# Attention scores in opposite 64-row halves, stacks filled head by head by transfers within SBUF, the maximum's row sent by ACT

## The reference

```
x = x + attention(layernorm(x))          # 16 heads of 16 channels, 512 tokens a sequence
q = xn @ Wq.T + bq + ocr_bias ; k = xn @ Wk.T + bk ; v = xn @ Wv.T + bv
scores = q @ k.T / 4 + band              # band: 0.1 where |i - j| <= 2
out = softmax(scores) @ v
return out @ Wo.T + bo
```

## Time and profile before

| | |
|---|---|
| Median of 3 runs | 4211.57 us (4206.95 to 4215.46) |
| The profiled execution | 4213.35 us, its span 4211.6 us |
| Attention stage, first to last score matmul | 2152.8 to 3442.4 us of the span |
| Busy: PE, PEld, DVE, ACT, POOL | 89%, 69%, 65%, 43%, 32% of the span |
| Exponential of one unit (ACT, line 1382) | mean 599 ns, 1024 times |
| Maximum of one unit (DVE, line 1476) | mean 687 ns, 1024 times |
| Band of one step (POOL, line 1134) | mean 1114 ns, 256 times |
| One low part (POOL, line 1143) | median 2416 ns, 32 times |
| Score matmuls (PE, lines 1217 and 1229) | mean 444 and 473 ns, 1024 times each |

### The profile page before, as it was taken

One profiled execution on the slowest core, in us unless ns is written; L12 is line 12 of the kernel. 1 busy time (PEld: TensorE's weight loads), 2 busy tenths in 40 slices (PEclk: granted clock), 3 DMA queues, 4 the chain that ended last, 5 costly groups with the idle time before them and its releaser, 6 DMA issues. The chain is left out here.

```text
span 4211.6 us, 79961 instructions
## 1 busy us (share of the span) xinstructions
PE 3768.9 (89%) x27516; PEld 2923.9 (69%) x27516; DVE 2720.6 (65%) x5626; ACT 1790.0 (43%) x3205; POOL 1364.4 (32%) x1045
## 2 busy tenths in 40 slices
PE   6997888887997999999968899998999979999999
PEld 4886677776886888888734455554555538888888
DVE  5665677775676566666655666666676655666665
ACT  3444344443554333333325555555555553333333
POOL 2555222222665222222222323323323322222222
PEclk9998999998998999999969999999999989999999
DMA  3000000000001000000034334333333410000000
GB/s 101 0 0 14 2 0 0 0 0 1 0 0 38 1 0 0 0 0 0 10 69 90 76 67 90 83 68 86 86 68 83 90 46 6 15 10 10 15 10 16
DMA packets 72273, 131.72 MB, mean 31 GB/s; under 512 B 7776, under 2 KB 40944, under 8 KB 66048
## 3 DMA queue, kind: packets, MB, share of 16 engines
q1 hardware_dynamic: 72192, 130.65, 13.2%
HBM read 71.38 MB, written 58.72 MB: 31 GB/s over the span
## 5 line engine op out<-in xcount | busy, mean ns | idle before, releaser
L1476 DVE TENSOR_REDUCE neg_max_sb<-s_ps 128x1 f32<-128x512 f32 x1024 | 689.5, 687 | 436.0 <-PE s_ps L1217 433.1
L1382 ACT ACTIVATE prob_sb<-s_ps 128x512 f32<-128x512 f32 x1024 | 599.8, 599 | 543.4 <-PE s_ps L1229 532.7
L850 POOL TENSOR_TENSOR m_act_lo_sb<-m_act_sb,m_act_hi_sb 128x512 fp32r<-128x512 f32 x320 | 414.1, 1294 | 1042.1 <-ACT m_act_hi_sb L816 1042.1
L806 ACT ACTIVATE m_silu_sb<-moe_h_ps 128x512 f32<-128x512 f32 x320 | 191.4, 598 | 966.7 <-PE moe_h_ps L761 966.7
L1229 PE MATMUL s_ps<-q_stack_sb,k_stack_sb 97*128 97x512 f32 x1024 | 483.3, 473 | 101.5 <-DMA q_stack_sb<-neg_max_t_sb 87.2
L1134 POOL TENSOR_TENSOR prob_sb<-prob_sb,band_sb 128x520 f32<-128x520 f32 (+1 forms) x256 | 285.2, 1114 | 853.0 <-ACT prob_sb L1382 852.9
L904 DVE TENSOR_TENSOR m_act_sb<-moe_h_ps,m_silu_sb 128x512 f32<-128x512 f32 x320 | 220.6, 689 | 502.1 <-ACT m_silu_sb L806 472.4
L1229 PEld LDWEIGHTS s_ps<-q_stack_sb,k_stack_sb 97*128 97x128 f32 x1024 | 203.0, 199 | 409.4 <-ACT prob_sb L1382 239.1
L1217 PE MATMUL s_ps<-k_stack_sb,q_stack_sb 96*128 96x512 f32 x1024 | 451.8, 444 | 28.7 <-DMA k_stack_sb<-qk_scratch 16.3
L529 POOL TENSOR_TENSOR f_sq_lo_sb<-f_sq_sb,f_sq_hi_sb 128x512 fp32r<-128x512 f32 x256 | 329.6, 1296 | 349.8 <-ACT f_sq_hi_sb L504 349.7
L916 DVE SCALAR_TENSOR_TENSOR x_resident_sb<-moe_y_ps,gates_sb,x_resident_sb 128x256 f32 (+1 forms) x1024 | 422.5, 474 | 0.5
(11 more groups left out here) (282 smaller groups left out, 8904.4 us busy)
## 6 DMA issues: line engine op xcount, KB each, us to landing
qk_scratch<-qk_hi_sb SPq DMA_DIRECT2D x128, 256.0 KB
q_stack_sb<-qk_scratch SPq DMA_DIRECT2D x64, 384.0 KB, 5.2
k_stack_sb<-qk_scratch SPq DMA_DIRECT2D x64, 384.0 KB, 7.0
qk_scratch<-qk_lo_sb SPq DMA_DIRECT2D x64, 256.0 KB
x_resident_sb<-x SPq DMA_DIRECT2D x4, 2048.0 KB, 17.8
out<-x_resident_sb SPq DMA_DIRECT2D x16, 512.0 KB, 2.9
moe_w_values_sb<-routed_w SPq DMA_DIRECT2D x12, 512.0 KB, 6.5
moe_w_values_sb<-shared_w SPq DMA_DIRECT2D x6, 256.0 KB, 5.4
```

The costliest lines, as they stand in the source:

```text
L850: nc.gpsimd.tensor_tensor(al[:, slot(e), :], act_f[:, e % 2, :], as_f32(ah[:, slot(e), :]), ALU.subtract).then_inc(low_ready, 1)
L1382: nc.scalar.activation(prob[:, kt % 2, i, :], s2p[i % 2][:, :], ACT.Exp).then_inc(exp_done, 1)
L1476: nc.vector.tensor_reduce(nm[:, g % 2, i, qt:qt + 1], s1p[i % 2][:, :], AXIS_X, ALU.max, negate=True).then_inc(max_done, 1)
```

## The change

- The stacks have 64 rows for a head: 48 of the operand, row 48 for the maximum, the rest zero. Groups 0 and 1 lie in rows 0 to 63, groups 2 and 3 in rows 64 to 127, two side by side in each half. The tensors `qs` and `ks` are half as large.
- The score matmuls read 48 rows (`s1_unit`) and 64 rows (`s2_unit`) of one half. The instruction built for such an operand addresses a 64 x 128 part of the array. AHEAD is 8 steps, two groups, so that the `s1` and the `s2` of a unit always lie in opposite halves.
- The detour through device memory is gone. SP copies from `qk_hi` and `qk_lo` to the stacks within SBUF (`to_stacks`), per head and slot: 16 rows of 2 KB, 24 transfers for a group and 96 for a sequence, in place of 20 larger ones. `qk_hi` and `qk_lo` hold both halves of the heads.
- The maximum's row is sent by ACT, right behind its copy, and no longer by SP.
- Pieces move: the transpositions to (1, 3) and (2, 0), the first half's projections to (3, 1), (3, 2), (3, 3) and (4, 0), its biases to (4, 1) and its high parts to (4, 2) and (4, 3).

```diff
-XT_AT = [(1, 2), (2, 1)]
-QK_AT = [[(3, 2), (4, 0), (4, 1), (4, 2)], [(8, 0), (8, 1), (8, 2), (9, 0)]]
+XT_AT = [(1, 3), (2, 0)]
+QK_AT = [[(3, 1), (3, 2), (3, 3), (4, 0)], [(8, 0), (8, 1), (8, 2), (9, 0)]]
 OT_AT = [(6, 1), (6, 2)]
 Y_AT = [(10, 0), (10, 1), (10, 2), (11, 0)]
 V_AT = [(13, 2), (14, 1), (15, 0), (15, 2)]
-AHEAD = 7
+AHEAD = 8
 STACK = 3 * HD
-MAX_ROW = 96
+HALF_ROWS = 64
...
-        qs = core.sbuf("q_stack", [P, GROUPS, GH, TOKENS], F32R, ctx)
-        ks = core.sbuf("k_stack", [P, GROUPS, GH, TOKENS], F32R, ctx)
+        qs = core.sbuf("q_stack", [P, GROUPS // KT, GH, TOKENS], F32R, ctx)
+        ks = core.sbuf("k_stack", [P, GROUPS // KT, GH, TOKENS], F32R, ctx)
...
-        qkh, qkl = (core.sbuf(n, [P, 2, TOKENS], F32R, ctx) for n in ("qk_hi", "qk_lo"))
-        bvs, bvl = qkh[:, :, 0:P], qkl[:, :, 0:P]
-
-        scratch = nc.dram_tensor("qk_scratch", (KT, 2, 3, HD, HEADS // KT, TOKENS), F32).ap()
...
-        PER_LOAD, PER_WRITE = 16 * 2, 16 * 6
+        PER_LOAD = 16 * 3 * GH
         first = lambda b: isinstance(b, int) and b == 0
+        def stack_rows(g, n):
+            return slice(HALF_ROWS * (g // 2), HALF_ROWS * (g // 2) + n)
...
-                def write(b, m, part, ready):
+                def to_stacks(b, g, part, ready):
+                    m = g // 2
                     sp.wait_ge(ready, KT * b + m + 1)
                     hold(sp, turns)
                     if part == 0 and not first(b):
-                        for g in (2 * m, 2 * m + 1):
-                            sp.wait_ge(loaded[g], PER_LOAD * b)
+                        sp.wait_ge(s2_ready, (b - 1) * STEPS * GH + TILES * GH * (g + 1))
                     src = (qkh, qkl)[part]
-                    for x, slots in enumerate((((0, 1), (0, 2)), ((2,), (1,)))[part]):
-                        for slot in slots:
-                            sp.dma_start(scratch[m, x, slot].rearrange("r h c -> h r c"),
-                                         as_f32(src[:, x, :])).then_inc(written[m], 16)
-                def load(b, g):
-                    m = g // 2
-                    sp.wait_ge(written[m], PER_WRITE * b + PER_WRITE)
-                    hold(sp, turns)
-                    if not first(b):
-                        sp.wait_ge(s2_ready, (b - 1) * STEPS * GH + TILES * GH * (g + 1))
-                    heads = slice(GH * (g % 2), GH * (g % 2) + GH)
-                    for x, stack in enumerate((qs, ks)):
-                        sp.dma_start(as_f32(stack[0:STACK, g, :, :]),
-                                     scratch[m, x, :, :, heads, :]).then_inc(loaded[g], 16)
-                def max_row(b, g):
-                    sp.wait_ge(nmt_ready, b * GROUPS + g + 1)
-                    sp.dma_start(as_f32(qs[MAX_ROW:MAX_ROW + 1, g, :, :]), as_f32(nmt[:, g % 2, :])).then_inc(rowed[g], 16)
-                for m in range(KT):
-                    write(0, m, 0, qkh_ready)
-                    write(0, m, 1, qkl_ready)
-                    load(0, 2 * m)
-                    load(0, 2 * m + 1)
-                max_row(0, 0)
+                    top = stack_rows(g, STACK).start
+                    for i in range(GH):
+                        head = slice(HD * (GH * (g % 2) + i), HD * (GH * (g % 2) + i + 1))
+                        for x, (stack, done) in enumerate(((qs, q_loaded[g]), (ks, k_loaded[g]))):
+                            for slot in (((0, 1), (0, 2)), ((2,), (1,)))[part][x]:
+                                rows = slice(top + HD * slot, top + HD * (slot + 1))
+                                sp.dma_start(as_f32(stack[rows, g % 2, i, :]),
+                                             as_f32(src[head, m, x, :])).then_inc(done, 16)
+                for g in range(GROUPS):
+                    to_stacks(0, g, 0, qkh_ready)
+                    to_stacks(0, g, 1, qkl_ready)
...
                 def body(b, before, more):
-                    max_row(b, 1)
                     if more:
-                        write(b + 1, 0, 0, qkh_ready)
-                        write(b + 1, 0, 1, qkl_ready)
-                    max_row(b, 2)
-                    if more:
-                        load(b + 1, 0)
-                        load(b + 1, 1)
-                        write(b + 1, 1, 0, qkh_ready)
-                        write(b + 1, 1, 1, qkl_ready)
-                    max_row(b, 3)
-                    if more:
-                        load(b + 1, 2)
-                        max_row(b + 1, 0)
-                        load(b + 1, 3)
+                        for g in range(GROUPS):
+                            to_stacks(b + 1, g, 0, qkh_ready)
+                            to_stacks(b + 1, g, 1, qkl_ready)
...
                 def low_part(b, m):
                     pool.wait_ge(qkh_ready, KT * b + m + 1)
-                    if m:
-                        pool.wait_ge(written[0], PER_WRITE * b + PER_WRITE)
-                    elif not first(b):
-                        pool.wait_ge(written[1], PER_WRITE * b)
-                    nc.gpsimd.tensor_tensor(qkl[:, :, :], full[:, :, :], as_f32(qkh[:, :, :]),
+                    if not first(b):
+                        for g in (2 * m, 2 * m + 1):
+                            pool.wait_ge(q_loaded[g], PER_LOAD * b)
+                            pool.wait_ge(k_loaded[g], PER_LOAD * b)
+                    nc.gpsimd.tensor_tensor(qkl[:, m, :, :], full[:, :, :], as_f32(qkh[:, m, :, :]),
                                             ALU.subtract).then_inc(qkl_ready, 1)
...
-                        pe.wait_ge(loaded[g], PER_LOAD * b + PER_LOAD)
+                        pe.wait_ge(q_loaded[g], PER_LOAD * b + PER_LOAD)
+                        pe.wait_ge(k_loaded[g], PER_LOAD * b + PER_LOAD)
                     pe.wait_ge(max_done, (b * STEPS + st) * GH + i + 1)
-                    r = slice(0, MAX_ROW)
-                    nc.tensor.matmul(s1p[i % 2][:, :], qs[r, g, i, qt * P:(qt + 1) * P], ks[r, g, i, :],
+                    r = stack_rows(g, STACK)
+                    nc.tensor.matmul(s1p[i % 2][:, :], qs[r, g % 2, i, qt * P:(qt + 1) * P], ks[r, g % 2, i, :],
                                      start=True, stop=True).then_inc(s1_ready, 1)
...
-                    r = slice(0, MAX_ROW + 1)
-                    nc.tensor.matmul(s2p[i % 2][:, :], ks[r, g, i, kt * P:(kt + 1) * P], qs[r, g, i, :],
+                    r = stack_rows(g, HALF_ROWS)
+                    nc.tensor.matmul(s2p[i % 2][:, :], ks[r, g % 2, i, kt * P:(kt + 1) * P], qs[r, g % 2, i, :],
...
                     nc.scalar.copy(nmt[:, g % 2, :], mp[0:TILES * GH, 0:P]).then_inc(nmt_ready, 1)
+                    act.wait_ge(nmt_ready, b * GROUPS + g + 1)
+                    row = stack_rows(g, STACK).stop
+                    act.dma_start(as_f32(qs[row:row + 1, g % 2, :, :]), as_f32(nmt[:, g % 2, :])).then_inc(rowed[g], 16)
...
-                            if more and (st, i) in ((4, 3), (9, 1)):
+                            if more and (st, i) in ((4, 1), (9, 1)):
                                 k_full(b + 1, st // 8)
...
-                            if more and (st, i) in ((5, 1), (5, 2), (9, 2), (9, 3)):
-                                high_part(b + 1, st // 8, int((st, i) in ((5, 2), (9, 3))))
+                            if more and (st, i) in ((4, 2), (4, 3), (9, 2), (9, 3)):
+                                high_part(b + 1, st // 8, int(i == 3))
...
-                            if more and (st, i) in ((4, 3), (9, 1)):
+                            if more and (st, i) in ((4, 1), (9, 1)):
                                 q_full(b + 1, st // 8)
```

More of the change, by code:

```diff
@@ L1023, in att_stage @@
         rowed = [s(f"{name}_max_row{g}") for g in range(GROUPS)]
-        loaded = [s(f"{name}_stack{g}") for g in range(GROUPS)]
-        written = [s(f"{name}_written{m}") for m in range(KT)]
+        q_loaded = [s(f"{name}_q_stack{g}") for g in range(GROUPS)]
+        k_loaded = [s(f"{name}_k_stack{g}") for g in range(GROUPS)]
         ot_ready = s(name + "_ot_ready")
@@ L1367, in high_part @@
                         act.wait_ge(full_ready, 2 * (KT * b + m + 1))
-                        if m:
-                            act.wait_ge(written[0], PER_WRITE * b + PER_WRITE)
-                        elif not first(b):
-                            act.wait_ge(written[1], PER_WRITE * b)
-                    op = nc.scalar.copy(qkh[:, x, :], full[:, x, :])
+                        if not first(b):
+                            for g in (2 * m, 2 * m + 1):
+                                act.wait_ge(q_loaded[g], PER_LOAD * b)
+                                act.wait_ge(k_loaded[g], PER_LOAD * b)
+                    op = nc.scalar.copy(qkh[:, m, x, :], full[:, x, :])
                     if x:
```

6 lines of the change are left out of this document (4 added, 2 removed).

## The result

The changed kernel takes 4290.32 us in the median (4281.97 to 4300.76, 4 runs), the kernel before 4213.31 in the same comparison: a ratio of 1.0187, 95% interval 1.0159 to 1.0214, clear of 1. It is slower by 77 us, where 4139 was forecast.

What follows compares the result with a forecast made beforehand. Prediction: PE waits for the late maximum's row and clock falls; plain steps are bound by the score-result-bank chain. −4.5 us a sequence, fifteen −67.5, start −5.4, end +1: −72, 4141.4 us (4139.5 against the median); range 4090 to 4235.

Steps and rivals of the forecast that it cites:

- copies to the stacks: SP's 24 small transfers a group within SBUF: a wait for group 0's stack at step 8, +0.9 us a sequence.
- p: Time SP takes for one small copy to the stacks, taken as 0.48 us; bounds 0.42 and 0.65.
- 24p − 10.6: Forecast wait in us for group 0's stack at step 8: 5.5 + 24p + 2.0 − 18.1, giving 0.9.
- Rival 1: SP too slow for its copies: 5.0 us wait at step 8, clock falls, +6.5 us a sequence, 4237 us; chance 0.15.
- Opposite halves: A unit's two scores overlap on PE, against added mode changes: net +1.7 us a sequence, bounds −2 and +9.
- rival 2: Score halves don't run side by side, or mode changes cost more: +7 us a sequence, 4245 us; chance 0.07.
- rival 3: PE's mode change mostly hidden and the issue fast: −2.7 us a sequence, 4098 us; chance 0.15.
- Rows sent by ACT: Maximum's row never late; steps 7, 8, 11, 12 shorter at full clock: −8.3 us a sequence, bounds −4.9 and −9.
- The issue on ACT: ACT issues the row four times a sequence ahead of an exponential: +0.4 us, bounds 0 and +2.2.
- The projections moved: Steps 3 and 4: projections wait behind `pv` or for the normalised input's low part: +0.8 us a sequence, bounds 0 and +2.
- Start: Before the loop: memset halved −3.4, first stack in 13.5 us −5.5, one more `s1` step +3.5; −5.4 us in all.

## Why the prediction was wrong

**The step that failed** is the term "copies to the stacks", +0.9, with its p = 0.48; all the copies cost 7.9 us a sequence (84.5 against 76.6 with half of them). The p was the pitch of small transfers at the program's start; the copies run at 0.63. The bounds held p too, but I took the nearest row by shape, 0.1 away from the 0.58 at which the gain is gone. Those rows are transfers from device memory. The prediction said that the trace had no small transfer within SBUF; it had one, the maximum's row itself, with 0.56 in the median, and I used it only for the upper bound and the rival.

The formula 24p − 10.6 gives 4.5 at the real p, and 3.9 was measured. It counts one p too many: landing is taken from the start of an issue, so that 23 pitches stand before it (5.3 + 14.5 + 2.2 − 18.1 = 3.9; the last copy starts at 2884.31, `s1` at 2886.50). And its 18.1 for steps 4 to 7 came out (18.06 in sequence 8) by luck: at full clock, with half of the copies, these steps take 17.0; the low clock in step 7 made them longer and hid a part of the wait.

**Rival 1** was therefore the mechanism, and its price nearly right: it put 6.5 us a sequence on top of the +0.9, and 7.0 came. Its parts were not: a wait of 5.0 where 3.9 was measured, and 2.4 for the clock where some 4 was lost. It let the clock fall behind the wait. In 13 of 15 periods it was down before, and the three projections of step 8 stand behind the wait: 13.38 us in sequence 8, which is 3.9 of waiting and 9.5 of work at 0.50 that takes 5.4 at full clock.

**Opposite halves**, +1.7, is the second term that failed: 5.4 us a sequence. The PE time behaved about as written and came out better, +0.6. A unit with a projection between its scores and the next, at full clock, first in halves and then over the full height:

```profile
2739.07 0.50 PE L1209 MATMUL s_ps<-q_stack_sb,k_stack_sb 64*128 64x512 f32 x1
2739.07 0.50 PE L1197 MATMUL s_ps<-k_stack_sb,q_stack_sb 48*128 48x512 f32 x1
2739.50 0.50 PE L1168 MATMUL tp_ps<-xnT_hi_sb,Wq_hi_sb 128*128 128x512 f32 x1
...
2740.39 0.49 PE L1209 MATMUL s_ps<-q_stack_sb,k_stack_sb 64*128 64x512 f32 x1
```

```profile
2779.86 0.40 PE L1210 MATMUL s_ps<-q_stack_sb,k_stack_sb 97*128 97x512 f32 x1
2780.10 0.40 PE L1198 MATMUL s_ps<-k_stack_sb,q_stack_sb 96*128 96x512 f32 x1
2780.33 0.40 PE L1169 MATMUL tp_ps<-xnT_hi_sb,Wq_hi_sb 128*128 128x512 f32 x1
...
2781.04 0.40 PE L1210 MATMUL s_ps<-q_stack_sb,k_stack_sb 97*128 97x512 f32 x1
```

The two scores start together, which excludes rival 2. The piece follows 0.43 later, where it follows the last score by 0.23 over the full height: 0.2 for this change of mode, as forecast, which excludes rival 3. The whole unit takes 1.32 for 1.18, so +0.14 where the formula has −0.24 + 0.42 = +0.18; the two changes together cost 0.38 for 0.42.

What was missing is a term for the clock, 4.8 us a sequence. The prediction argued from the earlier trace rows that equally busy steps keep their clock, and those rows are of scores over 96 and 97 rows. The changed kernel's last sequence, at 0.84 where it was 1.00, shows it once more: +6.8 us from its first `s2` to its last (65.5 against 58.7), against the +1 forecast.

**Rows sent by ACT**, −8.3. The step times were right (4.41, 5.19; in the changed kernel 4.08 and 3.59 at steps 11 and 12), and so was the term where nothing else is late: with the issue on ACT −7.9, and the kernel with tall stacks and half of the copies takes 72.1 us a sequence for 80.2. The sum for the kernel before alone was not: 29 us for 118, since a wait for the stack stood right behind. The prediction said of this edit "with nothing in front of it the row is never late", but not what is late next.

**The issue on ACT** took 0.52 and showed no loss that could be told apart. **The projections moved**: the wait for the low part came (19.0 us in all, 1.3 each), and step 3 fell to clock 0.79, 8.31 us for 4.76; yet moving them back gained nothing, as the clock then fell elsewhere. The move is a gain of 0.9 us a sequence, where a loss of 0.8 was forecast. **Start**: 4.9 us earlier for 5.4; the first stack took 16.6 us for 13.5 (2128.74 to 2145.38), again by p.

**The sum again**, from the kernel before to the changed one by way of three of the runs. The 15 periods of two of them have not been shown yet, with the pieces back and half of the copies, and with half of the copies alone:

```profile
2168.30:3330.97 1162.67, 1076.22 (x5418) 473.25 (x5417) 793.12 (x1382) 668.76 (x1287) 369.63 (x284) 0.92 0.10 21
2165.54:3313.98 1148.44, 1046.75 (x5418) 470.23 (x5417) 792.23 (x1382) 665.08 (x1287) 370.24 (x284) 0.94 0.10 21
```

| us a sequence | from, to | forecast | measured |
|---|---|---|---|
| Row by ACT, waits and clock (with the lead of 8 and half of the copies) | 80.2, 72.1 | −7.9 | −8.1 |
| Opposite halves | 72.1, 77.5 | +1.7 | +5.4 |
| Pieces moved | 77.5, 76.6 | +0.8 | −0.9 |
| All the copies | 76.6, 84.5 | +0.9 | +7.9 |
| Sum | 80.2, 84.5 | −4.5 | +4.2 |

So the period is 8.7 us longer than forecast, 131 in fifteen; with 0.5 at the start and about 9 from the last sequence on, this is the 141 us between the forecast of 4141 and the profiled 4282. The rows are rounded, each kernel was profiled once, and the parts may depend on their order, since the clock answers to all of them at once. Only one was run in two orders: with all the copies the move gains 0.9 too (85.4 with the pieces back).
